# Sixteen steps per register load on TensorE in a graph kernel: the take pass and the adjacency build

## The reference, cut to what matters

```python
def _L0_gnn_ref(X, edge_row, edge_col, edge_val, W, b):
    msgs = edge_val[:, None] * X[edge_col]
    h = jax.ops.segment_sum(msgs, edge_row, num_segments=N_NODES)
    return h @ W.T + b
...
    x = _layernorm(x + _L0_gnn_ref(x, src, dst, edge_weight, L0_gnn_W, L0_gnn_b), axis=-1)
    x = _layernorm(x + _L1_gnn_ref(x, edge_attr_8, L1_gnn_Wq, L1_gnn_Wk, L1_gnn_Wv, L1_gnn_Wo, src, dst), axis=-1)
    x = _layernorm(x + _L2_gnn_ref(x, L2_gnn_relvectors, L2_gnn_w_ih, L2_gnn_w_hh, L2_gnn_b_ih, L2_gnn_b_hh, src, dst, edge_type_16), axis=-1)
    x = _layernorm(x + _L3_gnn_ref(x, edge_index, L3_gnn_W1, L3_gnn_b1, L3_gnn_W2, L3_gnn_b2, L3_gnn_fc1_w, L3_gnn_fc1_b, L3_gnn_fc2_w, L3_gnn_fc2_b), axis=-1)
```

## Time and profile before

| | |
|---|---|
| median of 3 runs | 3793.4 us (3788.97 to 3793.51) |
| the profiled execution's own time | 3787.5 us |
| its span in the profile | 3785.9 us, 53836 instructions |
| mean granted TensorE clock | 0.836 of full speed |
| TensorE matmuls busy | 2916.1 us (77%) |
| VectorE busy | 2178.6 us (58%) |
| GpSimd busy | 1629.3 us (43%) |
| take pass | about 800 to 1100 us of the span |
| build | about 2550 to 2910 us of the span |

### The profile page before, as it was taken

The page is one execution under the profiler, slowest core; times in us unless marked ns, Lnnn a source line. Parts: engine busy times, 40 slices in busy tenths (PEclk is TensorE's granted clock), DMA queues, the critical chain, the costliest instruction groups (busy, mean ns, idle before and its releaser), DMA issues.

```text
span 3785.9 us, 53836 instructions
## 1 busy us (share of the span) xinstructions
PE 2916.1 (77%) x10862; PEld 1831.7 (48%) x10863; DVE 2178.6 (58%) x7167; ACT 680.5 (18%) x1768; POOL 1629.3 (43%) x1961
## 2 busy tenths in 40 slices
PE   2157777757778777777688877877777999999998
PEld 1133434435546444444476766642333666455754
DVE  5856666634443588888788888767775000543002
ACT  0012222200013222222100000015552000452000
POOL 0057777754320477777577777500000222001443
PEclk6578898889999888888677677657788999999999
DMA  2034322247641344443433333403332444003887
GB/s 95 33 77 112 108 101 101 101 129 199 192 125 44 84 106 107 107 106 106 74 99 103 102 103 104 77 2 124 126 126 88 146 139 142 1 1 106 276 268 231
DMA packets 317488, 423.25 MB, mean 112 GB/s; under 512 B 182634, under 2 KB 227888, under 8 KB 317014
## 3 DMA queue, kind: packets, MB, share of 16 engines
q0 software_dynamic: 105264, 324.88, 28.8%
q1 hardware_dynamic: 208024, 92.58, 9.4%
q10 hardware_dynamic: 3982, 3.24, 0.3%
HBM read 312.03 MB, written 112.79 MB: 112 GB/s over the span
## 4 chain that ended last, share of the span: by engine, by line
PE 43%; DVE 17%; DMA 13%; POOL 12%; issue 11%; ACT 2%; SPq 1%; DVEq 1%; POOLq 0%; ACTq 0%
PE PSA L846 14%; POOL G L450 7%; PE PSA L810 7%; DMA tab_m<-G,posi 6%; PE PSA L969 5%; PE PSA L833 5%; POOL tab_m L432 4%; DMA G<-tab_k,srci 4%; DVE S L1524 3%; PE PSA L1024 2%; DMA G<-tab_v,srci 2%; DVE S L1525 1%; DMA G<-tab_m 1%; PE PSA L923 1%; PE PSA L805 1%
## 5 line engine op out<-in xcount | busy, mean ns | idle before, releaser
L468 POOL DMA_DIRECT2D G<-tab_A x375 | 201.4, 538 | 1110.3 <-PE PSA L846 644.8
L432 POOL DMA_INDIRECT tab_m<-G,posi x448 | 436.4, 974 | 353.3 <-DVE G L1268 267.3
L450 POOL DMA_INDIRECT G<-tab_k,srci x448 | 426.2, 951 | 306.0 <-DMA tab_v<-KV 169.8
L450 POOL DMA_INDIRECT G<-tab_v,srci x448 | 439.7, 981 | 165.3 <-issue 96.6
L864 PE MATMUL PSA<-ident,oh 128*128 128x128 f32 x896 | 309.1, 345 | 232.2 <-DVE oh L1237 228.5
L969 PE MATMUL PSA<-work,oh 128*128 128x256 f32 x896 | 418.2, 560 | 46.9 <-DVE work L1452 32.0
L602 ACT COPY ohT<-PSA 128x128 f32<-128x128 f32 x896 | 237.5, 265 | 1062.6 <-PE PSA L864 1039.6
L1237 DVE TENSOR_SCALAR oh<-iota_f,dstl 128x128 f32<-128x128 f32 x1344 | 413.9, 309 | 5.5 <-DVE near L1373 0.5
L873 PE MATMUL PSA<-X,ohT 128*128 x896 | 349.4, 481 | 43.7 <-DVE G L1266 22.6
L923 PE MATMUL PSA<-Q,ohT 128*128 x896 | 365.6, 500 | 15.8 <-ACT ohT L602 8.0
L864 PEld LDWEIGHTS PSA<-ident,oh 128*128 128x128 f32 x896 | 143.8, 160 | 471.8 <-DVE oh L1237 448.0
(11 more groups left out here) (315 smaller groups left out, 4118.5 us busy)
## 6 DMA issues: line engine op xcount, KB each, us to landing
G<-tab_A POOLq DMA_DIRECT2D x375, 320.0 KB
tab_A<-G SPq DMA_DIRECT2D x125, 320.0 KB, 2.1
G<-tab_m SPq DMA_DIRECT2D x224, 129.0 KB, 2.6
G<-tab_m POOLq DMA_DIRECT2D x224, 129.0 KB
WT<-tab_m SPq DMA_DIRECT2D x544, 1.0 KB
rec<-tab_rec SPq DMA_DIRECT2D x448, 6.5 KB
tab_m<-G,posi POOLq DMA_INDIRECT x448
G<-tab_k,srci POOLq DMA_INDIRECT x448
```

What stands on the lines that cost most here:

```text
L432: pool.indirect_dma_start(tab_m[0:E, :], bass.IndirectOffsetOnAxis(ap=posi[:, t:t + 1], axis=0), G[:, t % GR, :MW], None, bounds_check=E - ...
L450: pool.indirect_dma_start(G[:, t % GR, :p.w], None, p.table, bass.IndirectOffsetOnAxis(ap=srci[:, t:t + 1], axis=0)).then_inc(p.rows[t % G ...
```

## The change

TensorE loads registers at every sixteenth step in both stages, 32 values at a time. The number of build steps is rounded up to a multiple of 16; it was 544 and stays 544. Both one-hot matrices of the build have sixteen buffers; those of `ohd` move from the scratch tensor `S` to `Q`, which is free at that time. VectorE waits only from step 16 on, and for the step 16 before.

```diff
-    T2 = -(-(-(-E // P) + NK - 1) // U) * U
+    T2 = -(-(-(-E // P) + NK - 1) // GRP) * GRP
...
-        ohd = S[:, 3 * T2:3 * T2 + 4 * GW // 2].bitcast(BF16).rearrange("p (r n) -> p r n", n=GW)
-        o2 = 3 * T2 + 4 * GW // 2
-        ohs = S[:, o2:o2 + U * P // 2].bitcast(BF16).rearrange("p (r n) -> p r n", n=P)
+        ohd = Q[:, 0:GRP * GW // 2].bitcast(BF16).rearrange("p (r n) -> p r n", n=GW)
+        ohs = S[:, 3 * T2:3 * T2 + GRP * P // 2].bitcast(BF16).rearrange("p (r n) -> p r n", n=P)
...
                 for t in range(T):
                     r = t % U
-                    if r == 0:
+                    if t % GRP == 0:
                         _, at = nc.values_load_multi_w_load_instructions(
-                            tz[:, 2 * t:2 * (t + U)], engines=[ET.PE], min_val=0, max_val=512 * (SLOTS + 3),
+                            tz[:, 2 * t:2 * (t + GRP)], engines=[ET.PE], min_val=0, max_val=512 * (SLOTS + 3),
...
-                    tile, slot = at[2 * r:2 * r + 2]
+                    tile, slot = at[2 * (t % GRP):2 * (t % GRP) + 2]
...
             for t in range(T2):
-                if t % U == 0:
+                if t % GRP == 0:
                     _, at = nc.values_load_multi_w_load_instructions(
-                        kz[:, 2 * t:2 * (t + U)], engines=[ET.PE], min_val=0, max_val=1024 * (SLOTS - 1),
+                        kz[:, 2 * t:2 * (t + GRP)], engines=[ET.PE], min_val=0, max_val=1024 * (SLOTS - 1),
...
-                pe.matmul(PSA[:, bass.ds(slot, GH)], ohs[:, t % U, :], ohd[:, t % 4, 0:GH],
+                pe.matmul(PSA[:, bass.ds(slot, GH)], ohs[:, t % GRP, :], ohd[:, t % GRP, 0:GH],
...
             def ends(t, r, turn):
                 pair = pairs(t)
-                dve.wait_ge(b_step, t + 5)
-                dve.tensor_scalar(ohd[:, r % 4, :], iota_h, pair[:, 1:2], None, ALU.is_equal).then_inc(b_oh, 1)
+                if t >= GRP:
+                    dve.wait_ge(b_step, U + t - GRP + 1)
+                dve.tensor_scalar(ohd[:, r, :], iota_h, pair[:, 1:2], None, ALU.is_equal).then_inc(b_oh, 1)
```

More of the change, by code:

```diff
@@ L148, in gnn_kernel @@
     assert NB % GT == 0 and NK <= P
-    T2 = -(-(-(-E // P) + NK - 1) // U) * U
+    T2 = -(-(-(-E // P) + NK - 1) // GRP) * GRP
     T2H = T2 // 2
-    assert T2H <= 512
+    assert T2H <= 512 and T2 % GRP == 0
     SCALE = float(DH) ** 0.5
@@ L322, in gnn_kernel @@
         sk = S[:, 2 * T2:3 * T2].bitcast(I32)
-        ohd = S[:, 3 * T2:3 * T2 + 4 * GW // 2].bitcast(BF16).rearrange("p (r n) -> p r n", n=GW)
-        o2 = 3 * T2 + 4 * GW // 2
-        ohs = S[:, o2:o2 + U * P // 2].bitcast(BF16).rearrange("p (r n) -> p r n", n=P)
-        assert o2 + U * P // 2 <= T * H
+        ohd = Q[:, 0:GRP * GW // 2].bitcast(BF16).rearrange("p (r n) -> p r n", n=GW)
+        ohs = S[:, 3 * T2:3 * T2 + GRP * P // 2].bitcast(BF16).rearrange("p (r n) -> p r n", n=P)
+        assert 3 * T2 + GRP * P // 2 <= T * H and GRP * GW // 2 <= NB * D
         iota_h = gru[:, 0:GW // 2].bitcast(F16)
@@ L1014, in _ @@
             for t in range(T2):
-                if t % U == 0:
+                if t % GRP == 0:
                     _, at = nc.values_load_multi_w_load_instructions(
-                        kz[:, 2 * t:2 * (t + U)], engines=[ET.PE], min_val=0, max_val=1024 * (SLOTS - 1),
+                        kz[:, 2 * t:2 * (t + GRP)], engines=[ET.PE], min_val=0, max_val=1024 * (SLOTS - 1),
                         skip_runtime_bounds_check_because="both columns are clamped when the table is made",
                         bass_reorder=False)
-                k, slot = at[2 * (t % U):2 * (t % U) + 2]
+                k, slot = at[2 * (t % GRP):2 * (t % GRP) + 2]
                 pe.wait_ge(b_ev, k & 255)
@@ L1023, in _ @@
                 settle(pe)
-                pe.matmul(PSA[:, bass.ds(slot, GH)], ohs[:, t % U, :], ohd[:, t % 4, 0:GH],
+                pe.matmul(PSA[:, bass.ds(slot, GH)], ohs[:, t % GRP, :], ohd[:, t % GRP, 0:GH],
                           start=False, stop=True, skip_group_check=True)
-                pe.matmul(PSA[:, bass.ds(slot + 512, GH)], ohs[:, t % U, :], ohd[:, t % 4, GH:GW],
+                pe.matmul(PSA[:, bass.ds(slot + 512, GH)], ohs[:, t % GRP, :], ohd[:, t % GRP, GH:GW],
                           start=False, stop=True, skip_group_check=True).then_inc(b_step, 1)
@@ L1522, in ends @@
                 pair = pairs(t)
-                dve.wait_ge(b_step, t + 5)
-                dve.tensor_scalar(ohd[:, r % 4, :], iota_h, pair[:, 1:2], None, ALU.is_equal).then_inc(b_oh, 1)
+                if t >= GRP:
+                    dve.wait_ge(b_step, U + t - GRP + 1)
+                dve.tensor_scalar(ohd[:, r, :], iota_h, pair[:, 1:2], None, ALU.is_equal).then_inc(b_oh, 1)
                 dve.tensor_scalar(ohs[:, r, :], iota_h[:, 0:P], pair[:, 0:1], None, ALU.is_equal).then_inc(b_oh, 1)
             for t in range(T2):
-                ends(t, t % U, t // U)
+                ends(t, t % GRP, t // GRP)
             for i in range(7):
```

## The result

The changed kernel takes 3805.2 us, median of 15 runs (3793.05 to 3817.33); the kernel before takes 3789.9 us (15 runs, 3780.09 to 3797.13). The ratio is 1.0046 with a 95% interval of 1.0033 to 1.0058: some 15 us slower. The forecast was 3805.

A forecast was written before the change was run, and what follows sets the result against it. The prediction took TensorE's sequencer to bound the build and a slot's lap the take pass. Build -8, lap +10 and clock falls +10 made +12 us on 3793.4, so 3805 us, range 3783 to 3832 (forecast's own 3797 to 3822).

The forecast's parts named there:

- The price of the load: TensorE, both stages: a register load of 32 values takes 2.13 us, against 1.105 for sixteen.
- the rival of a cheap load: Both stages: a 32-value load costs less than estimated, giving 3778 us at 1.83 or 3765 at 1.5; chance 0.08.
- The take pass, its lap: +10: Take pass: the load is hidden in a slot's lap only every other time, costing 10 us over 27 pairs.
- The R of 5.10: Take pass: the lap of a slot, from one step to the next in it, lasts 5.10 us.
- the formula R + 5.47: Take pass: a pair of turns lasts one slot's lap plus 3.44 plus 2.03 us, against two laps before.
- the other bound: Take pass: a turn paced by TensorE alone takes 4.44 us, 3.44 of steps and 1.0 of exposed load.
- The clock falls: +10 for five: Take pass: longer idle times before every second turn make the clock fall five times, about 2 us each, 10 us.
- The rival in which the clock falls nearly every time: Take pass: 15 to 27 clock falls cost 30 to 54 us, giving 3825 to 3849 us; chance 0.13.
- The build: -8: Build: half as many loads save 6.5 us, and fewer slow-load extras 1.5, making it 8 us shorter.
- The buffers at nothing: Build: sixteen one-hot buffers instead of four change nothing, as TensorE never waits for VectorE there.
- the rival of the buffers: Build: the repeating gap is a lack of one-hots that sixteen buffers close, some -46 us, 3747; chance 0.04.
- A wash: Whole kernel: no clock falls and laps of 5.24 us or more, giving 3785 to 3791, up to 3797; chance 0.19.

The follow-up runs named there:

- e1: Only the take pass changed (32-value loads at every sixteenth step), build as in the kernel before: 3800.7 us, ratio 1.0039 to the kernel before.
- e11: Only the take pass changed (32-value loads at every sixteenth step), run again in another session: 3804.1 us, ratio 1.0057 to the kernel before.
- e4: Only the take pass changed, plus a spare matmul before each of its register loads: 3799.4 us, ratio 1.0033 to the kernel before.
- e12: Only the take pass changed, plus a spare matmul before each load, run again in another session: 3794.1 us, ratio 1.0036 to the kernel before.
- e6: Kernel before with sixteen slots of G and 32-value loads at every sixteenth step in the take pass: 3716.8 us, ratio 0.9817 to the kernel before.
- e5: Kernel before with sixteen slots of G instead of eight in the take pass, loads still every eighth step: 3715.2 us, ratio 0.9821.
- e2: Only the build and its buffers changed, take pass as in the kernel before: 3784.8 us, ratio 0.9997 to the kernel before.
- e7: Kernel before with every finished cell of the build stored twice, the second copy to an unread table: 3817.6 us, one execution.
- e9: Changed build, take pass as before, each finished cell's store cut from 640 to 16 columns: 3761.7 us, one execution.
- e8: Kernel before with sixteen one-hot buffers in the build, 16-value loads kept at every eighth step: 3782.0 us, ratio 0.9999 to the kernel before.

## Why the prediction was right, point by point

**The total** came out within 1 us of the forecast, and that closeness is luck. The sum was -8 + 10 + 10 = +12 on the kernel before. Measured is +15.3: nothing in place of the -8, and 15.3 (e1) or 22.8 (e11) in place of the +20 of the take pass. And the kernel before came out 3.5 us lower in 15 runs than in the three shown.

**The price of the load**, 2.13 us, is right: 2.134 in the take pass. With it falls the rival of a cheap load.

**The take pass, its lap: +10.** Right in cause; the size is partly luck. Nearly without falls the pass is 11 to 15 us longer (e4, e12). The model gave 10.57 us for a pair and 10.20 before; whole passes give 11.1 to 11.3 (312.1 and 315.8 over 28) and 10.76. Both sides are half a microsecond or more too low. The R of 5.10 came from two single laps. With the pass's own 301.3 / 56 = 5.38 the formula R + 5.47 gives 10.85 for a pair, 0.09 more than two turns and 2.4 us in all, so it leaves out part of what a pair costs. That the lap is the cause is shown by e6: with the lap out of the way the same loads cost nothing. What I had wrong is the other bound, a turn paced by TensorE alone. I put it at 4.44 us with 1.0 of the load exposed; it is 4.17 with sixteen slots (e5), as most of a load is covered where matmuls are queued.

**The clock falls: +10 for five.** That the loads' idle time makes them is shown by the spare matmul, which takes the falls behind loads away. The profiled execution of the change had six falls behind loads, that of e1 five, that of e11 three; the rest, as before, follow waits for data. A fall read directly costs 1.3 us, not 2. Six of them are 8 us; with the lap's 11 to 15 that is 19 to 23 of the 27.1 us by which the pass of the slowest run grew, and what the rest is stays open. The falls' share in a usual run isn't settled: 1.3 us by one pair of medians and 10.0 by the other. The rival in which the clock falls nearly every time is out: 8 falls for 28 loads at most.

**The build: -8.** This is the term that failed; measured is 0 (e2). I took half of the slow loads' extra time to go with half of the loads, though of these I had written "I know no cause for that". The cause is that a store under way lengthens a load (e7, e9), and a load twice as long meets one more often: 28 of 34 took over 2.4 us in the change, where 20 of 68 had taken over 1.3. The extra over the least length was 82.6 - 68 x 1.102 = 7.7 us before (I had reckoned with 20 x 0.26 = 5.2) and 85.0 - 34 x 2.128 = 12.6 after: 4.9 more, where I had 1.5 less. That is 6.4 of the 8 us; the rest is inside the 6 us that I had allowed for the clock. The two parts of the sum that I could work out from rows, fewer fixed costs and a load of 2.13, agree with e9, where no store lengthens a load.

**The buffers at nothing** is right (e8), and the rival of the buffers is out with it; the earlier trace rows had said so.

**A wash** is out: its 3797 at most lay 0.1% above the median it started from, and measured is 0.33% to 0.58%.

What stays open: by what path a store holds up a register load, and why the first 110 us of the build had more long loads, with 117 GB/s there and 113 after; and the clock's share in a usual run. If the falls cost what the first session says, the lap is nearly all of the loss.

## What to carry to other kernels

A stall that is paid once per lap of a buffer ring may be free; put together with the next lap's, so that it comes at every other lap and is twice as long, it sticks out, because the ring can't hand on in one lap what it saved in another. Before a fixed cost is made rarer, ask what it hides behind now, and widen that first: the ring of 16 slots was worth 67 us and made the size of the load a matter of no account. And where a few instances of a cheap instruction are slower than the others for no known cause, find the cause before scaling them: here they grew when halved in number.

## What the runs showed of the hardware

- A register load on TensorE takes time nearly by the value: 0.590 us for 8, 1.105 for 16, 2.134 for 32, which is 64 ns for each further value.
- Stores that read SBUF lengthen it (a median of 1.11 to 1.57 us with stores doubled, none long with stores of 16 columns). The take pass's DMAs, which write SBUF, don't: in e6 its loads stay within 2.127 to 2.174 us at 256 GB/s. Whether the direction makes the difference, or something else in the stage, wasn't tried.
- In the three profiled executions with loads of 32 values, eight slots and no spare matmul, 14 of the 35 idle times of 1.85 to 1.88 us behind loads were followed by 1.2 GHz, and none of the 46 shorter ones. The clock also fell behind a wait for data of 1.05 us in e2 and one of 0.94 us in e9; from the idle time alone no single fall was to be foretold.
